# The first expert part routed in two halves, with the second half's chain between the first half's tiles

## The reference, cut to what matters

```python
x = x + 0.5 * ffn(layernorm(x))       # the first expert part, "f1"
x = x + attention(layernorm(x))       # 8 heads of 64, keys and values from a latent of 64
x = x + 0.5 * ffn(layernorm(x))       # the second expert part, "f2"

def ffn(x):                           # per token: one of 8 experts
    logits = x @ gate_w.T
    sel, rw = argmax(logits), sigmoid(max(logits))
    xs = x * rw                       # only to expert sel
    return (xs @ w_up[sel].T * silu(xs @ w_gate[sel].T)) @ w_down[sel].T
```

## Time and profile before

| | |
|---|---|
| time, median of 3 runs (lowest to highest) | 1071.98 us (1071.9 to 1072.31) |
| the profiled execution, own time | 1074.65 us |
| its span | 1072.8 us |
| busy: TensorE, VectorE, GpSimd, ScalarE | 90%, 65%, 64%, 44% |
| start, tiles, join of the first expert part, in the span | 0 to 58.1, 58.1 to 128.8, 128.8 to 147.9 us |
| the rest, attention and second expert part | 147.9 to 1072.8 us |

### The profile page before, as it was taken

The page is one execution under the profiler, slowest core; times in us unless marked ns, Lnnn a source line. Parts: engine busy times, 40 slices in busy tenths (PEclk is TensorE's granted clock), DMA queues, the critical chain, the costliest instruction groups (busy, mean ns, idle before and its releaser), DMA issues.

```text
span 1072.8 us, 14511 instructions
## 1 busy us (share of the span) xinstructions
PE 960.4 (90%) x5024; PEld 515.9 (48%) x5024; DVE 700.3 (65%) x1139; ACT 475.4 (44%) x765; POOL 686.5 (64%) x392
## 2 busy tenths in 40 slices
PE   6279966997999989999999999999999999896995
PEld 4168732443444454444445544444454444355884
DVE  4845468566778674776776566777666668676663
ACT  4824431443434435444543454444324444634663
POOL 0055350486989916677774577678637778885775
PEclk9679957798999999999999999999999999998998
DMA  9435421026011010000001000000100030005441
GB/s 328 157 108 160 131 74 69 6 78 176 11 15 16 11 69 1 1 1 1 1 1 69 1 1 1 1 1 1 69 2 1 1 118 1 1 34 189 138 140 48
DMA packets 39733, 59.92 MB, mean 56 GB/s; under 512 B 5866, under 2 KB 33518, under 8 KB 38640
## 3 DMA queue, kind: packets, MB, share of 16 engines
q1 hardware_dynamic: 17664, 25.14, 7.0%
q0 software_dynamic: 8736, 17.91, 6.1%
q10 hardware_dynamic: 13264, 15.97, 4.4%
HBM read 27.50 MB, written 25.85 MB: 50 GB/s over the span
## 4 chain that ended last, share of the span: by engine, by line
PE 64%; DVE 19%; POOL 7%; ACT 3%; issue 3%; DMA 2%; ACTq 1%; POOLq 0%; SPq 0%; DVEq 0%
PE ps_o L1290 15%; PE ps L1277 10%; DVE maxes L1113 8%; PE ps L1107 8%; PE ps L843 7%; DVE rows_store L1664 5%; PE ps_x L1087 5%; POOL arena_b L1766 4%; PE ps L1439 3%; PE ps_x L1312 3%; PE ps L827 2%; PE ps_o L859 2%; PE ps_x L859 1%; ACT rows_store L761 1%; DMA x_res<-x_in 1%
## 5 line engine op out<-in xcount | busy, mean ns | idle before, releaser
L1113 DVE TENSOR_REDUCE maxes<-ps 128x2 f32<-128x1024 f32 x256 | 310.7, 1217 | 196.9 <-PE ps L1107 196.3
L1766 POOL TENSOR_TENSOR arena_b<-arena_b 128x1024 f32<-128x1024 f32 x112 | 272.3, 2437 | 178.6 <-PE ps_o L1290 142.7
L1766 POOL TENSOR_TENSOR arena_b<-arena_b,hot_store 128x1024 f32<-128x1024 f32 x108 | 262.8, 2433 | 68.2 <-PE ps_o L1290 35.0
L1277 PE MATMUL ps<-q_split,keys_now 64*128 64x512 f32 x1536 | 205.3, 392 | 0.0
L1523 ACT ACTIVATE arena_b<-ps 128x1024 f32<-128x1024 f32 x144 | 143.3, 1023 | 101.6 <-PE ps L1277 101.6
L1277 PEld LDWEIGHTS ps<-q_split,keys_now 64*128 64x128 f32 x1536 | 145.3, 186 | 32.9 <-issue 4.1
L1290 PE MATMUL ps_o<-arena_b,latent_now 128*64 128x512 f32 x576 | 148.2, 616 | 1.3 <-ACT arena_b L1523 1.3
L1523 ACT ACTIVATE hot_store<-ps 128x1024 f32<-128x1024 f32 x112 | 112.0, 1022 | 57.5 <-PE ps L1277 57.5
L1290 PE MATMUL ps_o<-hot_store,latent_now 128*64 128x512 f32 x448 | 116.0, 614 | 2.5 <-ACT hot_store L1523 2.5
L1664 DVE RECIPROCAL rows_store<-rows_store 128x256 f32<-128x256 f32 (+1 forms) x72 | 112.6, 1564 | 6.5 <-ACT rows_store L1534 6.5
L1107 PE MATMUL ps<-keys_max_now,q_split 64*128 64x512 f32 x384 | 94.1, 486 | 7.6 <-DVE maxes L1113 6.4
(11 more groups left out here) (325 smaller groups left out, 1138.3 us busy)
## 6 DMA issues: line engine op xcount, KB each, us to landing
sorted_y<-arena_b ACTq DMA_DIRECT2D x40, 128.0 KB, 2.0
x_res<-sorted_x SPq DMA_DIRECT2D x32, 130.0 KB, 2.4
x_res<-x_in SPq DMA_DIRECT2D x4, 1024.0 KB, 13.8
scaled_x<-rows_store SPq DMA_DIRECT2D x16, 256.0 KB, 2.1
keys_now<-keys_next SPq DMA_DIRECT2D x4, 1024.0 KB, 4.5
sorted_x<-blank ACTq DMA_DIRECT2D x2, 1560.0 KB, 13.0
sorted_x<-blank ACTq DMA_DIRECT2D x2, 1430.0 KB, 10.2
arena_a<-w_gu SPq DMA_DIRECT2D x1, 2048.0 KB, 14.3
```

The source lines that it names most:

```text
L1113: nc.vector.tensor_reduce(maxes[:, 2 * m:2 * m + 2], bank[:, :, :], AX_X, ALU.max) \
L1277: last = nc.tensor.matmul(ps_s[n % 2][:, a, :], keys_now[h, key, k], query[h, p, q], start=False, stop=(kt >= KT - STRIDE and query is q_h ...
L1766: nc.gpsimd.tensor_tensor(t, t, prob(k, kt).rearrange("p a n -> p (a n)"), ALU.add) \
```

## The change

The first expert part is routed in two halves of 16 tiles, with the helpers of the second one. The first half's chain runs in the start: ScalarE and TensorE do it after the first six groups, and groups 6 and 7 and the second half's logits follow. The second half's chain stands between tiles: ranks on TensorE in tile 1, tokens in tile 10; on VectorE its instructions before tile 0 and in tiles 2 to 14; on ScalarE the exponential in tile 1, two row scalings in each of tiles 2 to 9, the scaled ids in tile 9. Each half has a DRAM table of rows and one of results. Each half's experts are rounded up by themselves, which makes 23 + 23 = 46 slot tiles. Hidden values and down products in f1 have one PSUM bank each, since ranks and tokens need the others, and `turn_hidden` and `down` wait accordingly. GpSimd's gathers of results stand behind its last gather of rows and wait for the first table only; VectorE takes the first seven in steps 43 to 49 of the tiles. The copies `ones_h` and `before_h` move from the join to the start.

```diff
 DONE = {"f1": 0, "f2": SLOT_TILES}
-TURN = {"a": 1, "b": 2}
+TURN = {"f1a": 1, "f1b": 2, "a": 3, "b": 4}
+BACK_AT = SLOT_TILES - 3
+RANKS_AT = 1
+TOKENS_AT = 10
...
-        scaled_x = nc.dram_tensor("scaled_x", [TOK, D], F32, kind="Internal").ap()
-        sorted_y = nc.dram_tensor("sorted_y", [SLOTS, D], F32, kind="Internal").ap()
+        scaled_x = [nc.dram_tensor(f"scaled_x{h}", [TOK // 2, D], F32, kind="Internal").ap() for h in range(2)]
+        sorted_y = [nc.dram_tensor(f"sorted_y{h}", [AHEAD_TILES * P, D], F32, kind="Internal").ap()
+                    for h in range(2)]
...
+            turn(0)
+            turn(1)
+            pe.wait_ge(sem("x_loaded1"), 16)
+            turn(2)
+            turn(3)
+            pe.wait_ge(sem("gate_ready"), 1)
+            logits_of(0)
+            pe.wait_ge(sem("x_loaded2"), 16)
+            turn(4)
+            logits_of(2)
+            turn(5)
+            back(0)
+            logits_of(4)
+            pe_ranks_late(pe, "f1a", AHEAD)
+            pe.wait_ge(sem("x_loaded3"), 16)
+            turn(6)
+            turn(7)
+            pe_tokens(pe, 0)
+            logits_of(6)
             back(1)
...
                         .then_inc(sem("x_copied"), 1)
-                if q == GROUPS - 1:
...
+            for q in range(4):
+                columns(q)
+            copy_rows(0)
+            act_std(act, "f1", 0, AHEAD)
+            columns(4)
+            columns(5)
+            act_exp_top_late(act, "f1a", 0, AHEAD)
+            for n in range(AHEAD_PAIRS):
+                act_scaled_pair(act, n)
+            columns(6)
+            columns(7)
+            act_hot_id(act, 0)
             copy_rows(1)
+            act_std(act, "f1", AHEAD, NT, 1)
...
-            dve_stats(dve, "f1", 0, NT)
+            stats_of(0)
+            stats_of(1)
+            dve_variance(dve, "f1", 0, AHEAD)
+            stats_of(2)
+            dve_scale(dve, "f1", 0, AHEAD, 0)
+            dve.wait_ge(sem("masks"), 3)
+            dve_logits(dve, 0)
+            dve_one_hot_late(dve, "f1a", 0, AHEAD)
+            dve.wait_ge(sem("x_tail"), 2)
+            dve_weight_late(dve, "f1a", 0, AHEAD)
+            dve_starts_late(dve, "f1a", 0, AHEAD, 0, small[:, 5, :])
+            dve.wait_ge(sem("tables"), 3)
+            dve_slots_late(dve, "f1a", 0, AHEAD)
+            dve_hot_hi(dve, 0)
+            dve_hot_lo(dve, 0, 0)
+            dve_hot_lo(dve, 0, 1)
+            stats_of(3)
+            dve_tokens(dve, 0)
+            dve_codes_early(dve, "f1", small[:, 5, :])
+            dve_variance(dve, "f1", AHEAD, NT)
...
+        def dve_hot_hi(dve, h):
...
+        def dve_hot_lo(dve, h, part):
...
+        def dve_tokens(dve, h):
...
-            nc.vector.tensor_copy(token_of[:, :], ids).then_inc(sem(f"token_of_{tag}"), 1)
-            return u
...
-            return banks[4 + k % 2 if tag == "f1" else 4][:, 0:P]
+        HID_BANK = banks[4][:, 0:P]
+        def down_bank(tag, k):
+            return banks[6 + k % 2 if tag == "f2" else 6][:, 0:D]
...
+        def pe_tokens(pe, h):
+            pe.wait_ge(sem("hot_id_f1"), 2 * h + 2)
+            for i in range(AHEAD):
+                if i % QT == 0:
+                    pe.wait_ge(sem("hot_lo_f1"), 2 * h + i // QT + 1)
+                last = nc.tensor.matmul(banks[4 + h][:, 0:2 * AHEAD_TILES], hot_lo[:, h * AHEAD + i, :],
+                                        hot_id[:, h, i, :, :].rearrange("p a h -> p (a h)"),
+                                        start=(i == 0), stop=(i == AHEAD - 1))
+            last.then_inc(sem("tokens_f1"), 1)
...
+        def act_scaled_pair(act, n):
+            act.wait_ge(sem("scale_late"), 2 * (n // AHEAD_PAIRS) + 2)
+            if n >= RING:
+                sent, count = rows_sent(n - RING)
+                act.wait_ge(sent, count)
+            for j in range(2):
+                t = 2 * n + j
+                nc.scalar.activation(rows_store[:, n % RING, j * D:(j + 1) * D], x_tile(t), ACT.Identity,
+                                     bias=x_all[:, t, SHIFT_AT:SHIFT_AT + 1],
+                                     scale=x_all[:, t, SCALE_AT:SCALE_AT + 1]).then_inc(sem("scaled_f1"), 1)
...
             for t in range(SLOT_TILES):
-                k = t % RING
+                h, k = t // AHEAD_TILES, t % RING
+                if t % AHEAD_TILES == 0:
+                    for n in range(RING):
+                        sent, count = rows_sent(h * AHEAD_PAIRS + AHEAD_PAIRS - RING + n)
+                        pool.wait_ge(sent, count)
+                    pool.wait_ge(sem("token_of_f1"), h + 1)
                 if t >= RING:
                     pool.wait_ge(sem("in_turned"), t - RING + 1)
-                pool.indirect_dma_start(rows_in[:, k, :], None, scaled_x[:, :],
+                pool.indirect_dma_start(rows_in[:, k, :], None, scaled_x[h][:, :],
                                         bass.IndirectOffsetOnAxis(ap=token_of[:, t:t + 1], axis=0)) \
-                    .then_inc(sem(f"in{k}_{tag}"), 16)
...
             def turn_hidden(t, k):
                 pe.wait_ge(sem("hid"), t + 1 + DONE[tag])
-                if old(t, 2) or tag == "f2" and t:
-                    pe.wait_ge(sem("hid_t"), t - (tag == "f1") + DONE[tag])
-                nc.tensor.transpose(hid_bank(tag, k), hidden[:, k % 2, :], ident[:, :]) \
+                if t:
+                    pe.wait_ge(sem("hid_t"), t + DONE[tag])
+                nc.tensor.transpose(HID_BANK, hidden[:, k % 2, :], ident[:, :]) \
                     .then_inc(sem("hid_turned"), 1)
             def down(t, k, e):
                 pe.wait_ge(sem("hid_t"), t + 1 + DONE[tag])
-                if old(t, 2):
-                    pe.wait_ge(sem(f"y_ready_{tag}"), t - 1)
-                nc.tensor.matmul(banks[6 + k % 2][:, 0:D], hidden_t[:, k % 2, :], dn_rows[:, ds(e * D, D)],
+                if tag == "f1" and t:
+                    pe.wait_ge(sem("y_ready_f1"), t)
+                if tag == "f2" and t >= 2:
+                    pe.wait_ge(sem("y_ready_f2"), t - 1)
+                nc.tensor.matmul(down_bank(tag, k), hidden_t[:, k % 2, :], dn_rows[:, ds(e * D, D)],
                                  start=True, stop=True).then_inc(sem("down"), 1)
...
                     down(t - LAG, (k - LAG) % RING_2, digits[k % RING])
                 if k % RING == 2 and ahead:
-                    if tag == "f2" and t // RING + 1 == EARLY_GROUPS:
-                        pe.wait_ge(sem("tile_expert_f2"), 2)
...
                     turn_hidden(t - 1, (k - 1) % RING_2)
+                if tag == "f1":
+                    inside(t)
+            def inside(t):
+                if t == RANKS_AT:
+                    pe_ranks_late(pe, "f1b", AHEAD)
+                if t == TOKENS_AT:
+                    pe_tokens(pe, 1)
             pe.wait_ge(sem(f"experts_loaded_{tag}"), 32)
...
+            def inside(t):
+                if t == 1:
+                    act_exp_top_late(act, "f1b", AHEAD, NT)
+                if 2 <= t < 2 + AHEAD_PAIRS:
+                    act_scaled_pair(act, AHEAD_PAIRS + t - 2)
+                if t == TOKENS_AT - 1:
+                    act_hot_id(act, 1)
             if tag == "f2":
...
+            def inside(t):
+                if t == -2:
+                    dve_scale(dve, "f1", AHEAD, NT, 1)
+                elif t == -1:
+                    dve_logits(dve, 1)
+                    dve_one_hot_late(dve, "f1b", AHEAD, NT)
+                elif t == 2:
+                    dve_weight_late(dve, "f1b", AHEAD, NT)
+                elif t == 3:
+                    dve_starts_late(dve, "f1b", AHEAD, NT, 0, small[:, 6, :])
+                elif t == 4:
+                    dve_slots_late(dve, "f1b", AHEAD, NT)
+                elif t == 5:
+                    dve_hot_hi(dve, 1)
+                elif t in (6, 8):
+                    dve_hot_lo(dve, 1, (t - 6) // 2)
+                elif t == TOKENS_AT + 1:
+                    dve_tokens(dve, 1)
+                elif t == TOKENS_AT + 2:
+                    dve_counts_late(dve, small[:, 5, :], small[:, 6, :])
+                elif t == TOKENS_AT + 4:
+                    dve_codes_late(dve, "f1")
+                elif BACK_AT <= t:
+                    dve_gathered(dve, (t - BACK_AT) // RING, (t - BACK_AT) % RING)
...
-            for k in range(RING):
-                pool.wait_ge(sem(f"y_stored{k}_f1"), 16 * (SLOT_TILES // RING))
+            for t in range(AHEAD_TILES - RING, AHEAD_TILES):
+                sent, count = y_sent(t)
+                pool.wait_ge(sent, count)
             for t in range(JOINED):
...
         def pool_join(pool, t):
-            pool.indirect_dma_start(x_tile(t), None, sorted_y[:, :],
+            pool.indirect_dma_start(x_tile(t), None, sorted_y[1][:, :],
...
             act.wait_ge(sem("row_scale_att"), 2)
+            for t in range(SLOT_TILES - RING, SLOT_TILES):
+                sent, count = y_sent(t)
+                act.wait_ge(sent, count)
...
```

(2 more changed lines are left out.)

325 lines of the change are left out of this document (109 added, 216 removed).

## The result

The changed kernel takes **1084.12 us** (median of four runs, 1083.91 to 1084.64), the kernel before 1072.14 in the same comparison: slower, a ratio of 1.0113 with a 95% interval of 1.0095 to 1.013. I had forecast 1075.5 and a range up to 1080.5, so the sign was right and the size wrong by 8.6 us.

A forecast was written before the change was run, and what follows sets the result against it. Start, TensorE-bound tiles and join hang end to end, so changes there show one for one. -11.3 + 5.4 + 1.1 + 9.75 + 1.0 - 2.5 = +3.45, rounded +3.5, on 1071.98: 1075.5 us, range 1069.8 to 1080.5.

The forecast's parts named there:

- The start: Up to tile 2's gate-up: first tile at 47.3 us instead of 58.1; start and first tiles together -11.3 us.
- The insertions: Tiles 2 to 9: the second half's routing pieces, mostly on VectorE, between tiles delay TensorE, +5.4 us.
- the 2 and 11 of the bounds: Tiles 2 to 9: routing pieces cost 2 us if each hid like its twins, 11 if none hid anything.
- The tokens: Tile 10: the second half's tokens on TensorE, 16 small multiplications, +1.1 us.
- The step that failed: First expert part's tiles: one bank for the down product leaves 0.4 us spare, nothing paid in steady state.
- The six tiles: First expert part: six more slot tiles at 1.625 us each, +9.75 us.
- The drain: Last gate-up to fold: three down products wait for ScalarE, VectorE adds gathered rows; +1.0 us, between 0 and 3.
- The join: Fold to attention's first transposes: fold, table load and normalization bind instead of gathers, 17.0 us for 19.1; counted -2.5.
- a rival for a clock that stays up: Fold and join: clock stays up through both, 5.6 us less, time 1069.9; chance 0.16.

The follow-up runs named there:

- the drain filled: Changed kernel with six added products, results unread, two ahead of each of the last three down products of the first expert part: 1080.99 us, ratio 1.0095.
- the kernel with four edits: Changed kernel with two down banks from tile 4, second routing chain cut smaller, root inside the fold, six unread products before the last three down products: 1070.5 us.
- the kernel before with its drain filled: Kernel before with six added products, results unread, in front of its last three down products, in a free bank: 1074.05 us, ratio 1.0013.

## Why the prediction was wrong

- **The start came out as forecast, by luck in part.** Gate-up of tile 2 at 50.7 instead of my 53.9, against a base that itself was 2.9 long in the first profile: -11.4 against -11.3. Two errors hide in that agreement. In this profile the clock was full again at 41.3 us, so the last logits took 2.9 instead of 3.7 and the rows were turned at 43.98 and not at 47.3, outside the 45 to 50 that I had given; and the base's first tile was 2.2 late. And the profile is the fastest of eleven there: with the middle one, 51.4, the row would be -10.7. In order of time, changed kernel, against the earlier trace rows:

```profile
39.26 2.91 PE L295 MATMUL ps_x<-arena_b,gate_c 128*32 128x512 f32 x8
43.98 0.41 PE L789 MATMUL ps<-ident,arena_b 128*128 128x128 f32 x2 [0.45 <-DMA arena_b<-scaled_x,token_of]
```

- **The insertions were right:** +4.6, forecast 5.4, between the 2 and 11 of the bounds; in the six other profiles with the single bank and the chain uncut 4.6 to 5.6. Some 0.6 of that is the single bank, by the kernel before with one (11.55 us for 10.94). Cutting the insertions smaller gave 2.1 back.
- **The tokens** agree by luck. The row has +1.2 for my 1.1, but the tokens moved the next gate-up by 0.4 us only, and 0.6 is the register load of the pace, met here too. My 1.1 came from 16 small products that I took for work at full clock; the clock was 0.50 there. At full clock the ranks' 16 took 0.70. The tokens and the load, changed kernel:

```profile
69.86 0.41 PE L789 MATMUL ps<-ident,arena_b 128*128 128x128 f32 x2 [0.47 <-issue]
70.11 0.27 PE L814 MATMUL ps<-ident,arena_b 128*128 128x128 f32 x1
70.22 0.56 PE L716 MATMUL ps<-hot_id,hot_store 128*128 128x46 bf16 x16
```

- **The step that failed** is the sentence "One bank for the down product: it is wanted at 70.51, the copy before it ends at 70.11, so 0.4 us are spare and nothing is paid in steady state". It cost 4.1 us in the steady tiles: 1.738 us a tile for 1.617. I compared when the bank is free with when the *array* wants it. The wait is met by the queue, which had run 1.5 us ahead, and its lead fell to 0.5 with a load of 1 us behind it. Restoring the second bank gave the pace back (1.631), and putting the single bank into the kernel before took it away (1.749). The six tiles themselves cost what I had said, 10.2 for 9.75 with the second bank back.
- **The drain** was mis-sized: +2.3, forecast +1.0. The three waits are there (0.66, 0.58, 0.74, where I had 0.4 each), the adds of VectorE that I had counted in are innocent. Changed kernel:

```profile
131.99 0.69 PE L823 MATMUL ps_o<-arena_a,arena_b 128*128 x2 [0.66 <-DVE arena_b L944]
133.38 0.69 PE L823 MATMUL ps_o<-arena_a,arena_b 128*128 x2 [0.58 <-DVE arena_b L944]
134.81 0.69 PE L823 MATMUL ps_o<-arena_a,arena_b 128*128 x2 [0.74 <-ACT arena_b L870]
```

- **The join is the second step that failed.** It had the wrong sign, +1.0 for -2.5. That the fold binds instead of the gathers was right (variance ready at 138.65, root at 153.68). But I took the fold's 13.0 us from the kernel before, where 5.3 of them were at full clock; here the clock fell 0.9 us in, and from the fold's start to the end of its last copy it took 16.4. I had a rival for a clock that stays up and none for one that falls sooner. With the drain filled the join is 16.5, and in the kernel with four edits, the root moved among them, 13.8. That a drain with idle brings the fall forward fits the profiles of the changed kernel and its variants, but not the kernel before with its drain filled; that cause stays open.
- The single bank thus sits in at least two rows of the ledger, pace and drain, and by the traces probably in the join. Alone it cost 7.9 us in the kernel before, and taking it out of the changed one gave 4.2 by the medians. So the rest of my sum was not right either: with the second bank back the time is 1079.95, 7.4 over the 1072.54 of the kernel before in the same comparison, where I had +3.5 for a bank that costs nothing. By that run's trace 2.6 of the difference are the join (+0.1 for -2.5) and 1.5 what lies before tile 9.

## What to carry to other kernels

A wait that is fulfilled before the product needs it need not be free: here it took away the lead of the engine's queue. Compare when the wait is passed with when the *queue* gets there, and look for what is slow in the queue behind it: a register load, an address to work out. When a stage gets new waits on TensorE, ask for the clock of the stage that follows, price it at both levels, and read it in more than one profile. And when a chain gets off the critical path, look at what stands in front of its consumer in program order: here the root waited 13.7 us behind copies that it didn't need.

## What the runs showed of the hardware

- TensorE's register load of one word from SBUF took 302 ns (median of 10) with the queue 1.5 us ahead of the array, 484 ns in the changed kernel; with the arithmetic and the check behind it, until the next wait in the queue, 0.65 and 1.0 us. It goes with the single bank and with nothing else of the change: in the kernel before with one bank it is 488, in the changed kernel with two 302. Changed kernel, kernel before, kernel before with one bank, changed kernel with two:

```profile
L797 PEldq TENSOR_LOAD <-tile_experts x10: 389/484/858, 60.7 to 125.3; - x10
L835 PEldq TENSOR_LOAD <-tile_experts x10: 295/302/312, 61.7 to 119.9; - x10
L835 PEldq TENSOR_LOAD <-tile_experts x10: 316/488/554, 61.8 to 125.2; - x10
L798 PEldq TENSOR_LOAD <-tile_experts x10: 296/302/571, 62.5 to 123.4; - x10
```

  Why the load itself is slower with the queue close to the array stays open.
- Six products of 128x128 by 128x256 that nobody reads made a kernel 3.1 us faster; in its profile the granted clock stayed at 2.4 GHz for 4.5 us more of what came behind. The same six made the kernel before 1.8 us slower, and its clock fell no later.
- The same kernel in two executions had its clock full from 41.3 us on, or at half for some 7 us from 46.3 and 3.4 us from 63.4 on. Its tile 11 came 3.3 us later there, 1.0 of it from a start that was late already. The kernel before spread over 1070.0 to 1075.2 us in all its runs.
